# The third value matrix of a step moves from ahead of the scores to behind them

## The reference

```
def attn_layer(x, Wqkv, qs, ksc, Wo):          # HEADS = 16, DIM_HEAD = 64, WINDOW = 32
    q, k, v = (sh(t) for t in jnp.split(x @ Wqkv, 3, -1))
    q, k = l2norm(q) * qs, l2norm(k) * ksc
    q = q * cos * scale + rotate_half(q) * sin * scale
    k = k * cos / scale + rotate_half(k) * sin / scale
    out = local_attention(q, k, v)             # each window of 32 sees itself and the one before
    return out.transpose(0, 2, 1, 3).reshape(b, n, INNER) @ Wo

for i in range(6):
    x = attn_layer(shift_tokens(x), ...) + x
    x = ffn_layer(shift_tokens(x), ...) + x    # (a * gelu(gate)) @ W2 behind a layer norm
```

## Time and profile before

| | |
|---|---|
| median of the runs | 1984.67 us |
| profiled execution | 1989.52 us, span 1987.7 us |
| TensorE matmuls | 1803.6 us busy, 91% |
| VectorE | 1534.6 us, 77% |
| ScalarE | 1366.4 us, 69% |
| GpSimd | 1266.6 us, 64% |
| granted TensorE clock, mean | 0.966 of full speed |

### The profile page before, as it was taken

How to read it: one execution, slowest core, us unless ns; L and a number is a source line. 1 busy time by engine, 2 the same in 40 slices (tenths; PEclk the granted TensorE clock), 3 DMA queues, 4 the chain that set the end, 5 groups by cost and what they waited for, 6 DMA issues and landing times. The chain is left out here.

```text
span 1987.7 us, 59622 instructions
## 1 busy us (share of the span) xinstructions
PE 1803.6 (91%) x24192; PEld 998.0 (50%) x24192; DVE 1534.6 (77%) x2549; ACT 1366.4 (69%) x2874; POOL 1266.6 (64%) x1127
## 2 busy tenths in 40 slices
PE   5898889668899999999999999999999999999974
PEld 3443444345455555555555555555555555555541
DVE  4778787347788888888888888888888888888833
ACT  1454444447787777887778877788777887778832
POOL 4303210238877877878778787787877778778710
PEclk8899999889999999999999999999999999999986
DMA  9000000323433334333343333433334333233300
GB/s 184 15 2 1 2 2 2 85 51 71 92 83 81 74 71 92 83 81 73 75 88 86 79 73 71 92 84 81 73 75 89 82 83 71 66 70 83 79 1 22
DMA packets 137216, 132.63 MB, mean 67 GB/s; under 512 B 79336, under 2 KB 82984, under 8 KB 136616
## 3 DMA queue, kind: packets, MB, share of 16 engines
q1 hardware_dynamic: 136944, 128.81, 29.2%
HBM read 20.94 MB, written 1.05 MB: 11 GB/s over the span
## 5 line engine op out<-in xcount | busy, mean ns | idle before, releaser
L1023 ACT ACTIVATE prob<-s_in,lower,rq 128x64 f32<-128x64 f32 x1536 | 535.2, 431 | 1.8 <-POOL lower L1191 1.6
L827 PE MATMUL bank_a<-x_shift,wqk_sb 128*128 128x512 f32 x768 | 368.0, 602 | 6.0 <-ACT sq L1136 4.2
L1009 ACT ACTIVATE zT<-bank_z 128x1024 f32<-128x1024 f32 x192 | 193.0, 1017 | 86.3 <-PE bank_z L838 86.3
L1162 POOL TENSOR_TENSOR prob<-prob,rden 128x1024 f32<-128x1024 f32 x96 | 182.9, 1905 | 96.8 <-DVE rden L1242 96.7
L827 PEld LDWEIGHTS bank_a<-x_shift,wqk_sb 128*128 128x128 f32 x768 | 146.3, 194 | 185.2 <-issue 178.1
L1181 POOL TENSOR_TENSOR kfin<-rk,kfin 128x512 f32<-128x512 f32 x96 | 122.4, 1275 | 174.4 <-ACT rk L1117 116.6
L384 ACT ACTIVATE a_prob<-a_sT 128x1024 f32<-128x1024 f32 x128 | 130.6, 1024 | 105.5 <-PE a_sT L218 103.4
L493 DVE TENSOR_REDUCE a_negmax<-a_max 128x1 f32<-128x512 f32 x256 | 164.7, 685 | 48.0 <-PE a_max L168 44.2
L846 PE MATMUL bank_y<-zT,wvo_high 128*128 128x512 f32 x384 | 187.9, 612 | 0.9 <-ACT zT L1009 0.9
L846 PE MATMUL bank_y<-zT,wvo_low 128*128 128x512 f32 x384 | 187.2, 610 | 0.6 <-ACT zT L1009 0.4
L838 PE MATMUL bank_z<-pT,xk_prev 32*128 32x128 f32 x3072 | 166.2, 285 | 16.5 <-DVE xn L1275 12.1
(11 more groups left out here) (176 smaller groups left out, 4009.8 us busy)
## 6 DMA issues: line engine op xcount, KB each, us to landing
kpad<-kfin SPq DMA_DIRECT2D x384, 128.0 KB, 2.4
qpair<-qfin SPq DMA_DIRECT2D x384, 128.0 KB, 2.4
wqk_sb<-in_wqkv SPq DMA_DIRECT2D x40, 128.0 KB, 2.7
xk_prev<-xk_own SPq DMA_DIRECT2D x24, 192.0 KB, 2.4
ffn_sb<-in_ffn SPq DMA_DIRECT2D x6, 537.5 KB, 4.3
wvo_low<-in_wqkv SPq DMA_DIRECT2D x6, 256.0 KB, 5.6
wvo_low<-in_wo SPq DMA_DIRECT2D x3, 512.0 KB, 6.7
wvo_high<-in_wqkv SPq DMA_DIRECT2D x6, 256.0 KB, 5.1
```

Source lines behind the costliest of these rows:

```text
L827: last = pe.matmul(bank_a[:, half, :], wqk_sb[:, layer_of(u) % 2, part, half, g * P:(g + 1) * P], cols(u), start=True, stop=True)
L1009: return act.activation(out, in_, ACT.Copy)
L1023: last = act.activation(prob[:, n % 2, i, :], s_in[:, n % 2, i, :], ACT.Exp, bias=lower[:, n % 2, i:i + 1], scale=rq[:, n % 2, i:i + 1])
L1162: pool.tensor_tensor(prob[:, e % 2], prob[:, e % 2], rden[:].unsqueeze(2).broadcast_to([P, TPB * GH, 2 * WIN]), ALU.mult).then_inc(pn_ok, 1)
```

## The change

Of the four value matrices of quarter h, the first two stay behind the key projection. The third is issued after the scores and before the key sums. The fourth stays where it was. No instruction is added or taken away, and no wait is added: the third has its waits behind it already, with the first two. In steps without quarter h nothing changes.

```
@@ -917,7 +917,7 @@
                     after(pe, z23_ok, h)
                     if h % GROUPS == 0:
                         after(pe, xa_ok, h // GROUPS - 1)
-                    project_out(h, 0, 3)
+                    project_out(h, 0, 2)
                 for stage, ok in ((GATE, gelu_ok), (LINEAR, hid_ok)):
                     v = unit_at(s - 1, stage)
                     if v is not None:
@@ -934,6 +934,8 @@
                     after(pe, qpair_in, c, 64)
                     after(pe, z01_ok, e - 1)
                     scores(c)
+                if quarter(h):
+                    project_out(h, 2, 3)
                 if quarter(n):
                     after(pe, sumk_ok, n)
                     after(pe, floorq_ok, c)
```

## The result

The changed kernel takes 2003.79 us in the median of nine runs (1995.94 to 2011.50), the kernel before 1984.84 (1978.17 to 1992.03, nine runs). The ratio is 1.0086, with a 95% interval from 1.0069 to 1.0104: slower by 0.9%, 19 us. The forecast was 1988 and no change that can be measured. The profiled execution took 2004.4 us, with a span of 2002.6 against 1987.7.

What follows compares the result with a forecast made beforehand. TensorE's own list was taken to bound nearly every step. The terms 0 + 0 + 0 + 3 + 0 gave +3 us on a median of 1984.67, so 1988 us, range 1976 to 2001.

Steps and rivals of the forecast that it cites:

- The bound: In nearly every step the length of TensorE's own list sets the step's end; its waits are 39 us in 1340.
- The wait before the key sums: TensorE's wait before L940, released by GpSimd's key squares whose chain has no scores result in it; unchanged, 0 us.
- Earlier scores: VectorE's 16.8 us wait for the query sums shortens, but the time is given back within the step; 0 us.
- the faster rival: Earlier scores reach the key sums' chain, so up to 28.7 + 6.8 us go: 1950; chance 0.06.
- Its weight load: The 0.1 us start cost of large matmuls passes from key sums to third matmul; 0, or 5 us either way.
- The waits for the transfers: TensorE before the scores: eleven steps with under 0.9 us to spare for the fourth qpair transfer wait 0.4 each; +3 us.
- The moderate form of the slower rival: Query-pair transfers land late in the 24 gate steps, 14 us, plus 3 in others: 17 us, 2002; transfers decide, chance 0.12.
- Instruction fetch: Fetch halts near the scores' end, in thirteen steps, keep their length though the steps hit can change; 0, -4 to +4.
- The range: 1976 to 2001: own bounds 1979 to 1997, widened by the slower rival above and the spread of runs below.

Runs made afterwards that it cites:

- the changed order with the shifted list: The changed kernel plus 33 tiny matmuls (132 records) at the head of TensorE's list, against the kernel before: 1998.22 us, ratio 1.0062.
- the change in those 20 steps alone: The change only in the 20 steps where an instruction block ends late in the scores, against the kernel before: 1997.48 us, ratio 1.0058.

## Why the prediction was wrong, point by point

*The bound: right.* TensorE's list sets the step. In undisturbed steps the four distances between key sums add up to 61.79 us before and to 61.78 in the changed order with the shifted list.

*The wait before the key sums, value 0: right.* The distance from the output step's key sums to the normalisation step's is 16.85 us, as before, and GpSimd's sum still releases them. 

*Earlier scores, value 0: right.* VectorE's wait for the query sums, 16.8 us before, is gone from the steady stretch, and what it waited for next grew instead:

```profile
DVE pq L1227 <- PE bank_a L827: 58.2, 65, 1.0
DVE den L1241 <- ACT prob L1025: 50.7, 44, 1.3
DVE rk L1272 <- PE bank_f L942: 38.5, 67, 2.4
```

The floor of the key sums waited 12.0 us before and 38.5 after. Nothing of the earlier scores reached the chain to the key sums; the faster rival did not come.

*Its weight load, value 0: right* within what can be told. Gate steps became 0.11 us longer (14.18 for 14.07) and output steps 0.11 shorter.

*The waits for the transfers, +3 us: right in kind, too small.* The profiled execution has 6.6 us of them. I counted eleven steps by the landings of one execution. SP's late issues fall in other steps in another execution: those with a wait were 8, 18, 24, 34, 38, 54, 58, 70, 74, 90 and 94 among others, and single ones lost up to 0.94 us. The moderate form of the slower rival is half true: its place and mechanism show, but with 7 us and not 17 it isn't what decided.

*Instruction fetch, value 0, bounds -4 to +4: wrong, and this is the step that failed.* I wrote that the scores and the query sums stay neighbours and "such a halt keeps its length". That holds only if the fetch starts earlier along with them. In the kernel before it looks so: the two stand within 0.3 us of each other in nine of the thirteen halting steps. In the changed kernel the fetch starts 0.4 to 1.5 us after the query sums in the halting steps from step 14 on. Counted from the key projection it starts where it did: 4.93 us before and 4.92 after in step 14, 4.25 and 4.28 in step 19, 4.34 and 4.40 in step 55, 3.77 and 3.80 in step 65, 4.28 and 4.35 in step 75. Of the nine steps from 14 on in which it starts late in both kernels, only step 50, with 5.61 and 5.09, is off by more than 0.2. The next block is then ready 1.2 to 1.6 us after that transfer's end in all kernels.

The records of TensorE's wait instructions (L725) show what the fetch stands behind. The last wait ahead of the scores, for the padded keys and query pairs, is taken up while value matmuls still run. It ends with the landing of the last query pair, or in the linear step just after the Gelu that the query sums ahead of it wait for. It ended 4.01 and 4.04 us after the key projection in step 14, 3.25 and 3.24 in step 55, 2.73 in step 65 of the changed kernel; the fetch started 0.92 and 0.88, 1.08 and 1.16, and 1.07 us after that. In the ten profiled executions with halts, 83 of the 92 halting steps from step 10 on have the fetch 0.9 to 1.2 us behind the end of this wait. The end of this wait stayed where it was, and the fetch with it. No run moved the wait alone; that it holds the fetch back is a close fit and not shown by an experiment.

The halts grew by 7.0 us in the profile; the change in those 20 steps alone costs 12.7 us. One execution can't tell two neighbours in time apart as causes; the row was priced as if it could.

The Trainium skill, page "Runtime: NRT & Kernel Launch", section "Instruction fetch mechanics", says that crossing a block is mostly hidden. The profiles do not agree for the scores: 12.1 us of halts before and 19.1 after. They agree with the same section on the block's size, 256 instructions: in all ten profiled executions with halts the stopped record stands at the same remainder of the count by 256, 192 or 193, depending on whether a wait instruction beside it is counted ahead of it.

*The range* held the bounds of each unknown separately. The upper end of 2001 came from the transfers alone; with the 7 us of the fetch on top it would have reached some 2008, and held the measured 2003.79.

## What to carry to other kernels

Work that stands ahead of a wait is cover for it, even when the trace shows no wait there: before moving it behind, list everything that must have arrived by then (transfers, a bank's last reader, and the next block of instructions), and ask of each whether it moves along or stays. Where a burst of tiny matmuls runs, look at what comes in the last microseconds ahead of it, and keep long matmuls there. A wait's cause is not settled by what starts beside it in one trace; a second order of the same work tells.

## What the runs showed of the hardware

A run of 128 matmul records of some 10 ns each, with as many weight loads, uses up 256 instructions in 1.3 us, while one 16 KB transfer of instructions mostly took 0.9 to 1.5 us and the block was ready another 1.2 to 1.6 us later. In every halt the scores went on 2.2 to 2.9 us after the transfer's start. So the scores halt if a block ends late in them and the transfer of the next starts less than that ahead.

With one long matmul between the query sums and the scores these transfers started earlier, 2.52 us after the key projection in step 19, 2.62 in step 55 and 2.50 in step 75, where it was 4.25, 4.34 and 4.28, and the halts vanished: in both profiled executions of that order no step from the fourth on has one above 0.1 us. The kernel with two matmuls at that place behaves the same but for one halt of 0.9 us.

Nor does every block's end late in the scores bring a halt. From step 10 on the twelve profiled executions have 210 steps in which a block ends within the last 25 of the 128 records. In 109 of them the next block's transfer started before the end of TensorE's last wait ahead of the scores, or with it, and one of these halted, for 0.2 us. In the other 101 it started 0.9 us or more behind that end, and 90 halted. In the order with one matmul behind the query sums all but one such step in each execution are of the early kind. What decides between the two, and why this order brings the early one, isn't shown by these runs. It stays open.
